# Second input transpose and third output product at other steps of the narrow attention

## The chip, the core and the metric

The kernel runs on one core of one Trainium2 chip. The metric is the device time of one execution, in microseconds (us). The core has a matmul engine (TensorE, PE in the rows; its weight loads are PEld), a vector engine (VectorE, DVE), a scalar engine (ScalarE, ACT), GpSimd (POOL) and SyncE (SP), which issues the DMAs. Each runs its own program in order; semaphores tie them together.

## The reference

Four transformer pieces one after the other on x (4 batches of 512 tokens, width 320) with a context of width 192. The change touches the attentions with 20 heads of 16 columns, which stand in the second piece (a self-attention and a cross-attention) and are the whole of the fourth piece:

```python
h1 = _ln(x, n1_g, n1_b)
x = _attn(h1, h1, q1, k1, v1, o1_w, o1_b, heads) + x
h2 = _ln(x, n2_g, n2_b)
x = _attn(h2, context, q2, k2, v2, o2_w, o2_b, heads) + x
...
q = (x @ wq).reshape(b, n, heads, dh).transpose(0, 2, 1, 3)
k = (ctx @ wk).reshape(b, j, heads, dh).transpose(0, 2, 1, 3)
v = (ctx @ wv).reshape(b, j, heads, dh).transpose(0, 2, 1, 3)
sim = jnp.einsum('bhid,bhjd->bhij', q, k) * scale
a = jax.nn.softmax(sim, axis=-1)
out = jnp.einsum('bhij,bhjd->bhid', a, v)
out = out.transpose(0, 2, 1, 3).reshape(b, n, heads * dh)
return out @ wo + bo
```

## The kernel before

The program is a row of stages: a wide attention (two stages, heads of 64), a feed-forward, the narrow attention of the second piece (two stages, run as one), a feed-forward, a gated attention, and the narrow attention of the fourth piece. `runs` makes two narrow runs: `Run("r3", ...)` with two stages of 4 batches, 8 units n = 0 to 7, and `Run("r7", ...)` with 4 units.

A narrow run is a software pipeline. The functions `narrow_pe`, `narrow_act` and `narrow_dve` each go through rounds n = -1 to N and in a round through 20 steps i (u = i // 4 is a group of four heads, kb = i % 4 a block of 128 keys). A round holds the work of three units: `now` (unit n: scores, exponentials, products with the values), `new` (unit n + 1: its input transposes and its projections) and `old` (unit n - 1: its output projection). A unit with both neighbours is called a full unit below; the first has no `old`, the last no `new`.

The pieces of a step, with the line of the instruction that shows in the trace:
- `cols_pe` (L958): the transposed scores of four heads, four matmuls side by side. It waits for the exponentials of the step before. `exp_act4` (L1003) makes the exponentials on ScalarE.
- `rows_pe4` (L975): scores the other way round, in bf16, of the step 6 later (`LEAD`), for the row maxima; called twice in each step (k = 0 and 1). Each call waits for the count `max`, that is for the VectorE reduction of the call before: `rows_dve4` (L990). Both calls write the same pair of banks.
- at kb = 1 `mix_pe4` (L1033), probabilities times values of the group before, with the first rows call inside; ScalarE copies it to `ox` (L1041). At kb = 2 `negm_pe4` (L1012), a transpose of the maxima, which `negm_dve4` (L1020) adds to the queries. At kb = 3 `turn_pe4` (L1048), transposes of `ox`, which `turn_dve4` reads (L1060, L1062).
- the inputs of the new unit: `T_pe4` (L1107), transposes of its normed (or plain) input in three parts T0, T1, T2, copied by `T_act4` (L1118 or L1120); for cross-attention `C_pe4` (L1129) with C0, C1.
- the output of the old unit: `out_pe4` (L1070), transposes in three parts, copied by `out_act4` (L1078); `y_pe4` (L1086), the output product of the token blocks y0 to y3, three matmuls each with 320 columns. `y_dve4` reads it with the bias added (L1092) and adds it to x (L1095).
- the projections of the new unit: `Q_pe4` (L1151) with the first rows call inside, `K_pe4` (L1178), `V_pe4` (L1204); `Q_act4` (L1160) reads Q0 with two activations.

Everything but the two kinds of scores goes through two PSUM banks, `M.XB` (bank6 and bank7). `step_items` lists the items in the order in which TensorE writes them, and `Turns.__init__` gives them the two banks in turn. So an item's matmuls wait (`wait_free`) until the item two places earlier in that list has been read. `wait_full` is the other direction: the reader waits for the matmuls. Which engine reads an item is fixed: VectorE reads negm, turn and y, ScalarE the others.

The order of the work inside a step is written out by hand, in `narrow_pe`, `narrow_act` and `narrow_dve`, and must agree with `step_items`.

Of the kernel before, what the change touches and what calls it, by code (L numbers as in the profile page):

```python
# [114 lines left out]
def program(nc, io):  # L115
    with ExitStack() as ctx:
# [159 lines left out]
        def overall(s, b):  # L276

            return b + (s.index * B - s.first)
# [140 lines left out]
        def x_ready(eng, s, b):  # L419

            eng.wait_ge(x_done, X_IN + (s.index * B + b) * TB - (B - 1) * TB)
# [482 lines left out]
        class Run(Turns):  # L904


            def step_items(self, n, i):

                u, kb = i // 4, i % 4
                items = []  # L910
                now, new, old = 0 <= n < self.N, n + 1 < self.N, 0 <= n - 1
                if i == 0 and now:
                    items += [("Q2", n), ("V3", n)]
                if kb == 1 and (old if u == 0 else now):
                    items += [("mix%d" % ((u - 1) % 5), n - 1 if u == 0 else n)]
                if kb == 3 and (old if u == 0 else now):
                    items += [("turn%d" % ((u - 1) % 5), n - 1 if u == 0 else n)]
                if i == 2 and now:
                    items += [("K2", n)]
                if i == 3 and new:  # L920
                    items += [("T0", n + 1)]
                if i == 4 and old:
                    items += [("out0", n - 1), ("out1", n - 1)]
                if i == 4 and new:
                    items += [("T1", n + 1)]
                if i == 6 and old:
                    items += [("out2", n - 1)]
                if i == 6 and new:
                    items += [("T2", n + 1)]
                if i == 7 and old:  # L930
                    items += [("y0", n - 1)]
                if i == 7 and new and self.cross[n + 1]:
                    items += [("C0", n + 1)]
                if i == 8 and new and self.cross[n + 1]:
                    items += [("C1", n + 1)]
                if i == 8 and old:
                    items += [("y1", n - 1), ("y2", n - 1)]
                if i == 11 and old:
                    items += [("y3", n - 1)]
                if new:  # L940
                    items += {10: [("Q0", n + 1)], 12: [("K0", n + 1)], 14: [("V0", n + 1)], 15: [("V1", n + 1)], 16: [("Q1", n + 1)],
                              18: [("K1", n + 1)], 19: [("V2", n + 1)]}.get(i, [])
                if kb == 2 and (new if u == 4 else now):
                    items += [("negm%d" % ((u + 1) % 5), n + 1 if u == 4 else n)]
                return items
# [152 lines left out]
        def T_pe4(pe, r, n, c):  # L1098
            (s, b), item, (a, w) = r.work[n], f"T{c}", CH3[c]
            r.wait_free(pe, item, n)  # L1100
            if c == 0 and s.prm["ln"]:
                pe.wait_ge(xn, TB * (overall(s, b) + 1))
            if c == 0 and not s.prm["ln"]:
                x_ready(pe, s, b)
            for t in range(TB):
                src = M.xn[:, t, a:a + w] if s.prm["ln"] else M.x[:, b * TB + t, a:a + w]
                last = nc.tensor.transpose(r.bank_of(item, n)[0:w, t * P:t * P + P], src, M.ident[:, :])  # L1107
            last.then_inc(r.full(item, n), 1)
# [108 lines left out]
        def narrow_pe(pe, r):  # L1217
            start(pe, r.work[0][0], r.work[0][1])
            for n in range(-1, r.N + 1):
                now, new, old = 0 <= n < r.N, n + 1 < r.N, 0 <= n - 1  # L1220
                for i in range(20):
                    u, kb = i // 4, i % 4
                    if now:
                        cols_pe(pe, r, n, i)
                    if i == 0 and now:
                        Q_pe4(pe, r, n, 2, n, i)
                        V_pe4(pe, r, n, 3)
                    elif i == 1 and old:
                        mix_pe4(pe, r, n - 1, 4, i)
                    elif kb == 1 and now and u:  # L1230
                        mix_pe4(pe, r, n, u - 1, i)
                    elif i == 2 and now:
                        K_pe4(pe, r, n, 2, n, i)
                    elif i == 3:
                        if old:
                            turn_pe4(pe, r, n - 1, 4)
                        rows_pe4(pe, r, n, i, 0)
                        if new:
                            T_pe4(pe, r, n + 1, 0)
                    elif i == 4:  # L1240
                        if old:
                            out_pe4(pe, r, n - 1, 0)
                            out_pe4(pe, r, n - 1, 1)
                        rows_pe4(pe, r, n, i, 0)
                        if new:
                            T_pe4(pe, r, n + 1, 1)
                    elif i == 6:
                        if old:
                            out_pe4(pe, r, n - 1, 2)
                        rows_pe4(pe, r, n, i, 0)  # L1250
                        if new:
                            T_pe4(pe, r, n + 1, 2)
                    elif i == 7:
                        if now:
                            turn_pe4(pe, r, n, 0)
                        rows_pe4(pe, r, n, i, 0)
                        if old:
                            y_pe4(pe, r, n - 1, 0)
                        if new and r.cross[n + 1]:
                            C_pe4(pe, r, n + 1, 0)  # L1260
                    elif i == 8:
                        if new and r.cross[n + 1]:
                            C_pe4(pe, r, n + 1, 1)
                        if old:
                            y_pe4(pe, r, n - 1, 1)
                        rows_pe4(pe, r, n, i, 0)
                        if old:
                            y_pe4(pe, r, n - 1, 2)
                    elif i == 10 and new:
                        Q_pe4(pe, r, n + 1, 0, n, i)  # L1270
                    elif i == 11:
                        if now:
                            turn_pe4(pe, r, n, 1)
                        rows_pe4(pe, r, n, i, 0)
                        if old:
                            y_pe4(pe, r, n - 1, 3)
                    elif i == 12 and new:
                        K_pe4(pe, r, n + 1, 0, n, i)
                    elif i == 14 and new:
                        rows_pe4(pe, r, n, i, 0)  # L1280
                        V_pe4(pe, r, n + 1, 0)
                    elif i == 15:
                        if now:
                            turn_pe4(pe, r, n, 2)
                        rows_pe4(pe, r, n, i, 0)
                        if new:
                            V_pe4(pe, r, n + 1, 1)
                    elif i == 16 and new:
                        Q_pe4(pe, r, n + 1, 1, n, i)
                    elif i == 18 and new:  # L1290
                        K_pe4(pe, r, n + 1, 1, n, i)
                    elif i == 19:
                        if now:
                            turn_pe4(pe, r, n, 3)
                        rows_pe4(pe, r, n, i, 0)
                        if new:
                            V_pe4(pe, r, n + 1, 2)
                    else:
                        rows_pe4(pe, r, n, i, 0)
                    if kb == 2 and u < 4 and now:  # L1300
                        negm_pe4(pe, r, n, u + 1)
                    if i == 18 and new:
                        negm_pe4(pe, r, n + 1, 0)
                    rows_pe4(pe, r, n, i, 1)

        def narrow_act(act, r):
            start(act, r.work[0][0], r.work[0][1])
            for n in range(-1, r.N + 1):
                now, new, old = 0 <= n < r.N, n + 1 < r.N, 0 <= n - 1
                for i in range(20):  # L1310
# [14 lines left out]
                    if i == 4 and old:  # L1325
                        out_act4(act, r, n - 1, 0)
                        out_act4(act, r, n - 1, 1)
                    if i == 4 and new:
                        T_act4(act, r, n + 1, 1)
                    if i == 6 and old:  # L1330
                        out_act4(act, r, n - 1, 2)
# [27 lines left out]
        def narrow_dve(dve, r):  # L1359
# [7 lines left out]
            for n in range(-1, r.N + 1):  # L1367
                now, new, old = 0 <= n < r.N, n + 1 < r.N, 0 <= n - 1
                norm = ln and n + 2 <= r.N
                for i in range(20):  # L1370
# [13 lines left out]
                    if i == 7 and old:  # L1384
                        s = r.work[n - 1][0]
                        dve.wait_ge(s.sem("cols_in"), 48 if s.prm["ln"] else 16)
                        y_dve4(dve, r, n - 1, 0)
                    if i == 8 and old:
                        y_dve4(dve, r, n - 1, 2)
                    if i == 11 and old:  # L1390
                        y_dve4(dve, r, n - 1, 3)
# [647 lines left out]
```

## Time and profile before

| | us |
|---|---|
| median of three runs | 3612.92 |
| lowest and highest run | 3609.6 and 3615.88 |
| profiled execution: measured time | 3612.91 |
| profiled execution: span from the first to the last instruction | 3611.0 |
| TensorE busy | 3419.9 (95%) |
| VectorE busy | 1909.7 (53%) |
| ScalarE busy | 1483.3 (41%) |
| GpSimd busy | 677.3 (19%) |

The run of 8 units begins with its first input transposes at 1923.3 us of the span and its last ones start by 2579.6; those of the run of 4 units lie between 3188.2 and 3437.2. In a timeline row the first number is the start, the second the length, both in us; several instructions of one kind that follow one another are one row, with their count. A bracket tells how long the engine had been idle and what ended that.

### The profile page before, as it was taken

To read this page: it belongs to the slowest core of one execution; us is meant where nothing else is said; L and a number is where in the kernel's file an instruction comes from. 1 tells how busy PE (TensorE), PEld (TensorE's weight loads), DVE (VectorE), ACT (ScalarE), POOL (GpSimd) and SP (SyncE) were. 2 spreads that over 40 slices of the span, in tenths; PEclk is the share of its full clock that TensorE was granted. 3 is DMA by queue.
4 is the path that set the end of the run, shared out by engine and by line. 5 is a ranking of instruction groups with operands and counts; after the bars stand their busy time and mean duration, and the time that the engine had idled before them with its cause. 6 is when DMAs were issued, how large, how long until landed. Compare 5 with 4: busy or idle time off the path is not lost.

```text
span 3611.0 us, 38848 instructions
## 1 busy us (share of the span) xinstructions
PE 3419.9 (95%) x15478; PEld 1418.8 (39%) x15478; DVE 1909.7 (53%) x2246; ACT 1483.3 (41%) x2023; POOL 677.3 (19%) x420
## 2 busy tenths in 40 slices
PE   8999999999999999999996899999998999989997
PEld 3334343433334343434443333333333545633332
DVE  3656556565656566661222666666661222556663
ACT  3443434344444535331110555556552112326553
POOL 2433333343333433330000000000000000000000
PEclk9999999999999999999997999999999999979999
DMA  3000000000100000002000000000003000000000
GB/s 109 19 15 15 19 15 15 21 17 21 33 18 15 21 12 15 15 1 57 0 0 24 1 1 1 21 10 5 1 1 80 1 0 23 1 5 5 5 1 30
DMA packets 43554, 60.49 MB, mean 17 GB/s; under 512 B 7408, under 2 KB 31216, under 8 KB 43376
## 3 DMA queue, kind: packets, MB, share of 16 engines
q1 hardware_dynamic: 43376, 58.02, 5.5%
q8 instruction: 124, 2.03, 0.2%
q14 instruction: 54, 0.44, 0.0%
HBM read 55.39 MB, written 2.62 MB: 16 GB/s over the span
## 4 chain that ended last, share of the span: by engine, by line
PE 89%; DVE 5%; issue 3%; ACT 2%; DMA 1%; SPq 1%; POOL 0%; ACTq 0%; DVEq 0%; POOLq 0%
PE bank L463 9%; PE bank L551 9%; PE bank L1033 6%; PE bank L673 5%; PE bank L348 5%; PE bank L1485 4%; PE bank L609 4%; PE bank L958 4%; PE bank L975 4%; PE bank L1487 4%; PE bank L1151 3%; PE bank L612 3%; DVE heads L990 3%; PE bank L644 2%; PE bank L1086 2%
## 5 line engine op out<-in xcount | busy, mean ns | idle before, releaser
L990 DVE TENSOR_REDUCE heads<-bank 128x2 f32<-128x1024 f32 x480 | 587.5, 1224 | 426.9 <-PE bank L975 425.7
L500 DVE TENSOR_REDUCE heads<-bank 128x2 f32<-128x1024 f32 x320 | 390.9, 1222 | 534.9 <-PE bank L488 531.2
L522 ACT ACTIVATE probs<-bank 128x1024 f32<-128x1024 f32 x320 | 327.6, 1024 | 425.8 <-PE bank L468 423.0
L535 POOL TENSOR_TENSOR heads<-heads,probs 128x1024 f32<-128x1024 f32 x160 | 381.2, 2382 | 254.8 <-ACT probs L522 252.2
L463 PE MATMUL bank<-heads 64*128 64x512 f32 x1280 | 361.3, 641 | 0.9 <-ACT probs L522 0.9
L551 PE MATMUL bank<-probs,values 128*64 128x512 f32 x1280 | 345.2, 618 | 0.2 <-ACT probs L522 0.2
L531 POOL TENSOR_TENSOR heads<-probs 128x1024 f32<-128x1024 f32 x80 | 193.1, 2413 | 749.2 <-ACT probs L522 749.2
L958 PE MATMUL bank<-heads 32*128 32x512 f32 x1920 | 306.5, 624 | 5.9 <-ACT weights L1003 3.0
L580 DVE RECIPROCAL rec<-ox 128x128 f32<-128x128 f32 x320 | 280.1, 917 | 7.7 <-ACT ox L573 7.7
L1003 ACT ACTIVATE weights<-bank 128x1024 f32<-128x1024 f32 x238 | 230.6, 1021 | 114.5 <-PE bank L958 113.9
L975 PE MATMUL bank<-heads 32*128 32x512 bf16 x960 | 191.7, 396 | 62.8 <-DVE heads L990 57.9
L1509 ACT ACTIVATE probs<-bank,b_col 128x512 f32<-128x512 f32 x80 | 55.0, 687 | 455.5 <-PE bank L1488 455.5
L1520 DVE SCALAR_TENSOR_TENSOR mixed<-bank,b_col,probs 128x512 f32<-128x512 f32 x80 | 60.0, 750 | 299.4 <-ACT probs L1509 299.4
L1169 POOL CAST heads<-heads 128x512 bf16<-128x512 f32 x60 | 36.2, 625 | 928.4 <-ACT heads L1160 928.4
L1003 ACT ACTIVATE probs<-bank 128x1024 f32<-128x1024 f32 x164 | 158.9, 1021 | 74.6 <-PE bank L958 73.9
L463 PEld LDWEIGHTS bank<-heads 64*128 64x128 f32 x1280 | 96.3, 184 | 223.0 <-issue 111.6
L348 PE MATMUL bank<-weights,mixed 128*128 128x320 f32 x640 | 173.7, 433 | 3.3 <-DVE mixed L1520 3.3
L975 PEld LDWEIGHTS bank<-heads 32*128 32x128 bf16 x960 | 46.0, 91 | 324.9 <-DVE heads L990 186.4
L586 DVE TENSOR_TENSOR mixed<-mixed,rec 128x512 f32<-128x512 f32 x62 | 168.4, 2716 | 0.1
L1485 PE MATMUL bank<-hT,weights 128*128 128x512 f32 x320 | 161.6, 628 | 6.2 <-DMA weights<-in_L_xattn_w_ff 3.1
L609 PE MATMUL bank<-hT,heads 128*128 128x512 f32 x320 | 160.1, 623 | 0.0
L1487 PE MATMUL bank<-hT,weights 128*128 128x512 f32 x320 | 152.5, 599 | 0.0
(202 smaller groups left out, 4819.2 us busy)
## 6 DMA issues: line engine op xcount, KB each, us to landing
heads<-in_wqk SPq DMA_DIRECT2D x40, 320.0 KB, 2.8
heads<-in_wqk SPq DMA_DIRECT2D x40, 256.0 KB, 2.6
ctx_in<-in_ctx SPq DMA_DIRECT2D x12, 384.0 KB, 3.7
weights<-in_L_xattn_wo SPq DMA_DIRECT2D x2, 1600.0 KB, 11.1
x_res<-in_x SPq DMA_DIRECT2D x4, 640.0 KB, 11.9
out<-x_res SPq DMA_DIRECT2D x1, 2560.0 KB, 8.7
weights<-in_L_xattn_w_ff SPq DMA_DIRECT2D x1, 1600.0 KB, 13.2
weights<-in_L_xattn_ff_w SPq DMA_DIRECT2D x1, 1600.0 KB, 14.5
```

Of the source, the lines that this page charges most:

```text
L348: last = nc.tensor.matmul(M.SM[t % 2][:, 0:D], v["OT"][:, c, t * P:t * P + P], v["wo"][:, c, :], start=c == 0, stop=c == NF - 1)
L463: nc.tensor.matmul(M.COLS[:, g, :], v["KT"][strip, U % 3, kb * P:kb * P + P], v["QT"][strip, U % 3, :], start=True, stop=False)
L500: nc.vector.tensor_reduce(v["negm"][:, U % 2, qb, :].rearrange("p (g k) -> p g k", g=2)[:, :, 0], M.ROWS[:, :, :], AX.X, ALU.max, negate=T ...
L522: nc.scalar.activation(v["probs"][:, kb, :, :], M.COLS[:, :, :], ACT.Exp, scale=float(r.work[n][0].prm["dh"]) ** -0.5).then_inc(r.sem("exp ...
L535: nc.gpsimd.tensor_tensor(ps, ps, pr[:, k, :, :], ALU.add).then_inc(r.sem("part"), 1)
L551: last = nc.tensor.matmul(M.WOB[64 * g:64 * g + 64, :], v["V"][:, kb, 2 * u + g, :], v["probs"][:, kb, g, :], start=kb == 0, stop=kb == TB ...
L609: last = nc.tensor.matmul(q[:, :], w[:, e, :], M.hT[:, e, :], start=False, stop=e == 1)
L958: last = nc.tensor.matmul(M.QUAD[:, g, :], v["KT"][strip, u, kb * P:kb * P + P], v["QT"][strip, u, :], start=True, stop=True)
L975: last = nc.tensor.matmul(M.ROWS4[:, j, :], v["QB"][strip, u, qb * P:qb * P + P], v["KB"][strip, u, :], start=True, stop=True)
L990: nc.vector.tensor_reduce(v["negm"][:, tile, qb, 64 * half:64 * half + 64].rearrange("p (g k) -> p g k", g=2)[:, :, at], M.ROWS4[:, :, :], ...
L1003: nc.scalar.activation(v["probs"][g % slots][:, 2 * h:2 * h + 2, :], M.QUAD[:, 2 * h:2 * h + 2, :], ACT.Exp, scale=float(r.work[n][0].prm[ ...
L1485: nc.tensor.matmul(gate[:, :], v["w1"][:, e, gf], M.hT[:, e, :], start=e == 0, stop=False)
```

## The change

The transposes T1 of the new unit are issued in step 5, behind the mix matmuls, instead of in step 4, behind the first rows call; their ScalarE copy moves with them. The output product y2 of the old unit is issued in step 10, behind the query projection and ahead of the negm transposes, instead of in step 8, between the two rows calls; on VectorE its two additions go from step 8 to step 10, behind the negm addition. `step_items` lists both at their new places, and with that the two banks change for the items between the old place and the new one. No operation is added or removed.

```diff
@@ step_items
-                if i == 4 and new:
+                if i == 5 and new:
                     items += [("T1", n + 1)]
...
                 if i == 8 and old:
-                    items += [("y1", n - 1), ("y2", n - 1)]
+                    items += [("y1", n - 1)]
...
+                if i == 10 and old:
+                    items += [("y2", n - 1)]
                 if kb == 2 and (new if u == 4 else now):
@@ narrow_pe
                         rows_pe4(pe, r, n, i, 0)
-                        if new:
-                            T_pe4(pe, r, n + 1, 1)
                     elif i == 6:
...
                         if old:
                             y_pe4(pe, r, n - 1, 1)
                         rows_pe4(pe, r, n, i, 0)
+                    elif i == 10:
+                        if new:
+                            Q_pe4(pe, r, n + 1, 0, n, i)
+                        else:
+                            rows_pe4(pe, r, n, i, 0)
                         if old:
                             y_pe4(pe, r, n - 1, 2)
-                    elif i == 10 and new:
-                        Q_pe4(pe, r, n + 1, 0, n, i)
...
+                    if i == 5 and new:
+                        T_pe4(pe, r, n + 1, 1)
                     if kb == 2 and u < 4 and now:
                         negm_pe4(pe, r, n, u + 1)
@@ narrow_act
-                    if i == 4 and new:
+                    if i == 5 and new:
                         T_act4(act, r, n + 1, 1)
@@ narrow_dve
-                    if i == 8 and old:
+                    if i == 10 and old:
                         y_dve4(dve, r, n - 1, 2)
```

What this does to the queues is shown for round n = 1 of the run of 8 units. In the new file the helpers' lines are 2 higher (L958 is L960, L975 is L977, L1086 is L1088, and so on), and L1398 is L1403. A row is an instruction of the queue, with its bank and the semaphores that it waits for; r3_free0 and r3_free1 count the readings of bank6 and bank7, r3_max the reductions.

TensorE, from the first rows call of step 4 to that of step 5, before:

```order
L975 MATMUL bank4<-heads 128x512 [waits r3_max]
...
L1107 MATMUL bank6<-ident,xn 106x128 [waits r3_free0]
L1107 MATMUL bank6<-ident,xn 106x128 x3
L975 MATMUL bank4<-heads 128x512 [waits r3_max]
...
L1033 MATMUL bank7<-weights,values 32x512 [waits r3_exp,r3_free0,r3_free1]
L1033 MATMUL bank7<-weights,values 32x512 x3
```

And now, to the end of step 5:

```order
L977 MATMUL bank4<-heads 128x512 [waits r3_max]
...
L1035 MATMUL bank6<-weights,values 32x512 [waits r3_exp,r3_free0]
L1035 MATMUL bank6<-weights,values 32x512 x3
...
L1035 MATMUL bank6<-mixed,values 32x512 x4
L1109 MATMUL bank7<-ident,xn 106x128 [waits r3_free1]
L1109 MATMUL bank7<-ident,xn 106x128 x3
L977 MATMUL bank4<-heads 128x512 [waits r3_max]
```

T1 has gone from between the two rows calls of step 4 to the end of mix0, and mix0 and T1 have changed banks.

TensorE in steps 10 and 11, from the query projection Q0 to y3, before:

```order
L1151 MATMUL bank6<-hT,weights 128x512 x2
L1012 MATMUL bank7<-ident,heads 128x128 [waits r3_max,r3_free1]
L1012 MATMUL bank7<-ident,heads 128x128 x3
L975 MATMUL bank4<-heads 128x512 [waits r3_max]
...
L1048 MATMUL bank6<-ident,ox 128x128 [waits r3_free1,r3_free0]
L1048 MATMUL bank6<-ident,ox 128x128 x3
...
L1086 MATMUL bank7<-weights,mixed 128x320 [waits s3_wo_in,r3_free0,r3_free1]
```

And now:

```order
L1153 MATMUL bank7<-hT,weights 128x512 x2
L1088 MATMUL bank6<-weights,mixed 128x320 [waits s3_wo_in,r3_free0]
L1088 MATMUL bank6<-weights,mixed 128x320 x2
L1014 MATMUL bank7<-ident,heads 128x128 [waits r3_max,r3_free1]
L1014 MATMUL bank7<-ident,heads 128x128 x3
L977 MATMUL bank4<-heads 128x512 [waits r3_max]
...
L1050 MATMUL bank6<-ident,ox 128x128 [waits r3_free0]
L1050 MATMUL bank6<-ident,ox 128x128 x3
```

y2 stands between Q0 and the negm transposes. The negm transposes now follow Q0 in bank7, and the turn transposes (L1050) follow y2 in bank6, where they followed Q0 before.

VectorE from the second rows call of step 10 to the first of step 11, before:

```order
L990 TENSOR_REDUCE heads<-bank4 128x2 [waits r3_rows]
L1020 TENSOR_TENSOR heads<-bank7,heads 128x512 [waits r3_q_cast,r3_full1]
L1398 BN_STATS stats<-x_res 128x6
L990 TENSOR_REDUCE heads<-bank4 128x2 [waits r3_rows]
L1060 RECIPROCAL rec<-bank6 128x16 [waits r3_free1,r3_full0]
```

And now:

```order
L992 TENSOR_REDUCE heads<-bank4 128x2 [waits r3_rows]
L1022 TENSOR_TENSOR heads<-bank7,heads 128x512 [waits r3_q_cast,r3_full1]
L1094 TENSOR_TENSOR ysum<-bank6,bo_row 128x320 [waits r3_full0]
L1097 TENSOR_TENSOR x_res<-ysum,x_res 128x320 [waits r3_free0]
L1403 BN_STATS stats<-x_res 128x6
```

The reading of y2 stands behind the reduction and behind the negm addition.

## Rows read from the trace of the kernel before

**Rows 1.** The page: the chain that ended last, by engine

```profile
PE 89%; DVE 5%; issue 3%; ACT 2%; DMA 1%; SPq 1%; POOL 0%; ACTq 0%; DVEq 0%; POOLq 0%
```

**Rows 2.** Stretches: us, then PE, PEld, DVE, ACT, POOL busy, clock, DMA

```profile
2100.00:2188.00 88.00, 84.06 (x520) 33.49 (x524) 59.05 (x77) 50.76 (x61) 6.60 (x12) 1.00 0.00 1
```

**Rows 3.** L1107 on PE: idle until, us in total, times

```profile
  ACT mixed L1078: 9.5, 8
```

**Rows 4.** Timeline of PE, round 1, steps 4 and 5

```profile
2102.32 1.15 PE L958 MATMUL bank<-heads 32*128 32x512 f32 x8
...
2105.98 0.65 PE L1107 MATMUL bank<-ident,xn 128*106 128x128 f32 x4 [1.18 <-ACT mixed L1078]
...
2106.57 1.24 PE L958 MATMUL bank<-heads 32*128 32x512 f32 x8
...
2111.77 1.24 PE L958 MATMUL bank<-heads 32*128 32x512 f32 x8
```

**Rows 5.** Timeline of PE, round 7 (no new unit), step 4

```profile
2659.94 1.14 PE L958 MATMUL bank<-heads 32*128 32x512 f32 x8
...
2663.74 0.39 PE L975 MATMUL bank<-heads 32*128 32x512 bf16 x2 [1.32 <-DVE heads L990]
```

**Rows 6.** Timeline of PE, round 0 (no old unit), behind T1 in step 4

```profile
2013.38 0.39 PE L975 MATMUL bank<-heads 32*128 32x512 bf16 x2 [0.75 <-DVE heads L990]
```

**Rows 7.** Timeline of PE and DVE, round 1, step 8

```profile
2123.30 0.39 PE L975 MATMUL bank<-heads 32*128 32x512 bf16 x2
...
2123.62 1.89 PE L1086 MATMUL bank<-weights,mixed 108*128 108x320 f32 x6
2123.73 1.23 DVE L990 TENSOR_REDUCE heads<-bank 128x2 f32<-128x1024 f32 x1 [0.84 <-PE bank L975]
2124.87 0.48 DVE L1092 TENSOR_TENSOR ysum<-bank,bo_row 128x320 f32<-128x320 f32 x1
...
2125.43 0.39 PE L975 MATMUL bank<-heads 32*128 32x512 bf16 x2
```

**Rows 8.** Timeline of all engines, round 1, steps 10 and 11

```profile
2133.19 1.98 PE L1151 MATMUL bank<-hT,weights 106*128 106x512 f32 x4
...
2135.01 0.60 PE L1012 MATMUL bank<-ident,heads 128*128 128x128 f32 x4
...
2135.30 1.44 ACT L1160 ACTIVATE heads<-bank,mask 128x512 f32<-128x512 f32 x2 [1.36 <-PE bank L1151]
...
2135.55 1.24 PE L958 MATMUL bank<-heads 32*128 32x512 f32 x8
2135.98 1.23 DVE L990 TENSOR_REDUCE heads<-bank 128x2 f32<-128x1024 f32 x1 [1.38 <-PE bank L975]
...
2136.80 0.66 PE L1048 MATMUL bank<-ident,ox 128*128 128x128 f32 x4
...
2137.12 0.68 DVE L1020 TENSOR_TENSOR heads<-bank,heads 128x512 f32<-128x512 f32 x1
...
2137.86 1.89 PE L1086 MATMUL bank<-weights,mixed 108*128 108x320 f32 x6
...
2139.68 1.24 PE L958 MATMUL bank<-heads 32*128 32x512 f32 x8
```

**Rows 9.** Timeline of PE, round 7, steps 10 and 11

```profile
2687.35 1.24 PE L958 MATMUL bank<-heads 32*128 32x512 f32 x8
...
2690.93 0.39 PE L975 MATMUL bank<-heads 32*128 32x512 bf16 x2 [0.80 <-DVE heads L990]
...
2695.05 1.24 PE L958 MATMUL bank<-heads 32*128 32x512 f32 x8
```

**Rows 10.** Round 0, step 9: the stretch, and timeline of PE

```profile
2029.00:2037.00 8.00, 7.88 (x48) 1.85 (x50) 2.52 (x3) 1.94 (x2) 0.00 (x0) 0.65 0.01 2
...
2029.13 2.31 PE L958 MATMUL bank<-heads 32*128 32x512 f32 x8
...
2036.91 1.24 PE L958 MATMUL bank<-heads 32*128 32x512 f32 x8
```

## The prediction

> **What bounds the kernel now.** I read the chain that ended last first: TensorE holds 89% of it [rows 1], so the kernel is one engine's program with holes, and a moved piece of TensorE work is worth what it does to the holes. The stretch-by-stretch view comes next: in a stretch of 88 us, about one middle unit of the narrow attention, TensorE is busy 84.06 us at a granted clock of 1.00, against 59.05 on VectorE and 50.76 on ScalarE [rows 2]. So nothing but TensorE has slack there, but TensorE's holes, some 4 us in a unit, are waits for the other two engines. Then I read one unit as a timeline. Its steps are counted by the scores matmuls (L958). Every step has two "rows" matmuls (L975), each answered by a reduction on VectorE (L990), and the second one has to wait for the reduction of the first. That pair is the second clock of a step: where little else stands between them, TensorE waits for VectorE; where much stands between them, it doesn't.
>
> Which units feel the change: T1 belongs to a unit that has a next one, y2 to a unit that has a previous one. The run of two attentions (8 units) has one unit with only a next (the first, beside a start-up round), six with both and one with only a previous; the run of the last attention (4 units) has one, two and one. So there are 8 full units, 2 first and 2 last ones. The wait list of T's line confirms the count: eight waits for a copy on L1078, 9.5 us together [rows 3].
>
> **Part 1, T1 leaves step 4.** Now step 4 lasts from 2102.32 to 2106.57, 4.25 us, and in it the transposes wait 1.18 us for ScalarE's copy of out0 [rows 4]. That wait goes, but not its whole length comes back, because the second rows matmul then waits for VectorE. The last unit of the run has no T1 and shows the same step without it: its second rows matmul starts 3.80 us after the scores and waits 1.32 us for VectorE [rows 5]; with 0.01 to the next scores the step is 3.81. So the gain is 4.25 - 3.81 = 0.44 us in each full unit, not 1.18 + 0.65. In a first unit there is no out0 and T1 stands beside the VectorE wait: its second rows matmul still waits 0.75 us behind T1 [rows 6], so nothing is gained there.
>
> **Part 2, T1 enters step 5.** It stands behind the last mix matmul and ahead of the second rows matmul. That step has no hole at its end: from 2106.57 to 2111.77 it lasts 5.20 us with no wait on the rows [rows 4]. So T1 costs its own time, 0.59 us (2105.98 to 2106.57) [rows 4], in full and first units alike. Its ScalarE copy comes after the copy of mix0 and ahead of the next exponentials, which by the same shift start later than the copy ends; I cost it at nothing. Bounds for this part: 0.59 to 0.65, the bare length of the four transposes.
>
> **Part 3, y2 leaves step 8.** Between the two rows matmuls of step 8 now stand the three y2 products: 2123.30 to 2125.43, 2.13 us. Without them the second waits for the reduction, which ends at 2123.73 + 1.23 = 2124.96; with 0.06 for the hand-over (as between ScalarE's end at 2136.74 and the transposes at 2136.80 [rows 8]) the start is 2125.02, a gain of 0.41 us out of 1.81 [rows 7]. The next reduction may not start earlier, as VectorE is by then at y1's two additions (from 2124.87) [rows 7], but the first mix matmuls of step 9 stand between it and the next rows matmul. The gain holds in 8 full and 2 last units.
>
> **Part 4, y2 enters step 10.** The step now is the query projection (L1151), the negm transposes (L1012) and the second rows matmul, back to back: 2133.19, 2135.01, 2135.55 [rows 8]. TensorE is the late one, so y2 costs what it takes in step 8: 2123.62 to 2125.43, 1.81 us [rows 7]. The order also makes negm3 share its bank with Q0. Q0 would be full 0.41 us earlier than now, so its two ScalarE passes end at 2135.30 + 1.44 - 0.41 = 2136.33, and y2 ends at 2135.01 - 0.41 + 1.81 = 2136.41. A tie: I take 0, and bound it by 0 to 0.3 us.
>
> **Part 5, step 11 gets a new wait.** With two banks in turn, an item waits until the item two places earlier has been read. Now turn1 follows Q0 in its bank, and ScalarE has read Q0 by 2136.74, when turn1 starts 1.25 us after the scores (2135.55 to 2136.80) [rows 8]. In the new order turn1 follows y2 in its bank, and y2 is read by VectorE, in the queue behind the second reduction of step 10 and the negm3 addition. Counted from the scores of step 11: reduction starts at +0.43 (2135.55 to 2135.98), negm3 addition +1.14 later (to 2137.12), then +0.60 (its 0.68 with the same 0.08 of overlap) [rows 8], the addition of y2 0.48 [rows 7], hand-over 0.06: 2.71 us. turn1 starts 1.46 us later than now. Behind it stand the first rows matmul, y3 and the second one. y3's present wait of some 0.15 us for the negm3 addition (2137.12 + 0.68 against its start at 2137.86) [rows 8] goes, so the step gets 1.46 - 0.15 = 1.31 us longer. The scores of step 11 are ahead of turn1, so ScalarE isn't starved, and nothing later in the unit is timed by anything but this chain; the delay stays.
> The Trainium skill, "PSUM — Partial Sum Buffer", section "Engine vs sequencer instructions", says that the VectorE queue is strict FIFO, which speaks against this place for y2. By that rule part 5 stands at 1.31; if VectorE could take y2 ahead of the waiting reduction it would be 0 and the time about 3627.7.
>
> **Sum.** Full unit: -0.44 + 0.59 - 0.41 + 1.81 + 1.31 = +2.86 us, times 8 = 22.9. First units: 0.59 x 2 = 1.2. Last units: -0.41, then step 10, where y2 first fills the 0.80 us that the second rows matmul waits there [rows 9], +1.81 - 0.80 = 1.01, then step 11 as before, from the same 4.12 us (2690.93 to 2695.05) [rows 9], +1.31: 1.91 x 2 = 3.8. Together +27.9 us. The profiled execution took 3612.91 us (span 3611.0), which is the median of the three runs, 3612.92; so the forecast is 3640.8 us, 0.77% slower.
>
> **Rivals.**
> *No wait in step 11.* If the hand-over of y2 to VectorE were not late (for instance if the reduction of step 10 is already done when turn1 comes), part 5 goes in 10 units: 27.9 - 13.1 = 14.8, so 3627.7. For it speaks only that such a wait isn't to be seen in the profile before; against it stands the order of VectorE's queue.
> *The moved work is hidden and the kernel gets faster.* This is the case if steps 5 and 10 have as much room on TensorE as the moved pieces take, 0.59 and 1.81 us, and y2 is read in time. Then only the gains are left: -0.85 x 8 - 0.41 x 2 = -7.6, so 3605.3. It decides at the point where another engine sets the length of those steps. The timeline speaks against it: TensorE's instructions follow one another there without a wait [rows 4, 8].
> *The clock falls.* In a first unit one step shows a granted clock of 0.65, so TensorE was for most of it at the lower of its two levels (1.2 and 2.4 GHz) [rows 10]: a step that normally lasts 5.20 us (2106.57 to 2111.77) [rows 4] took 7.78 (2029.13 to 2036.91) [rows 10], +2.58. If the new 1.46 us wait did this once in each full unit, it would add 20.6 us: 3661.4. Against it: full units have waits of 1.18 us now and run at 1.00 [rows 2, 4], and the new wait stands between busy steps. Where the clock falls already, in first and last units, the moment may shift; I allow one such step, 2.58 us, either way.
> The Trainium skill, "TensorE: Matmul & The Clock Gate", section "A second HAM failure mode: psum-queue depth-cycling", tells of a kernel whose short waits at PSUM banks made its clock swing between the levels; in this trace the full units, with waits of just that kind, don't.
>
> **How the numbers follow.** Forecast 0.82 (own range 3634 to 3647: the tie of part 4 up to +2.4, part 2 up to +0.6, the clock 2.6, and as much downwards for overlaps that I read too tightly); no wait in step 11 0.07; clock 0.05; faster 0.03; within 0.2% for reasons that I don't see 0.03. The range runs from 3627, to take in the first rival, to 3650, one or two falls of the clock beyond the forecast. Within 0.2%, 7 us, a measurement of this kernel can't tell a change from none. Faster 0.03, same 0.03, slower 0.94.
>
> **What the changed profile would show.** Right: T's line has no waits for L1078 left; step 4 of a full unit lasts 3.8 us and step 5 5.8; step 8 4.7 us instead of 5.1; step 10 6.7 instead of 4.9; step 11 5.4 instead of 4.1, with turn1 (the transposes of ox) waiting about 1.4 us for VectorE's y addition; a full unit grows by 2.9 us. Wrong: turn1 waits for ScalarE or not at all; the second rows matmul of step 8 moves by the whole 1.81 us; steps 5 and 10 keep their length; a granted clock under 1.00 in the middle units; or waits later in the unit that shrink by what step 11 lost.

## The result, and the profile after

The changed kernel takes 3642.22 us (median of 6 runs, 3639.7 to 3646.07) against 3612.72 us for the kernel before in the same rounds: a ratio of 1.0082 with a 95% interval of 1.0069 to 1.0095. It is slower, as forecast; 3640.8 us had been predicted. The profiled execution's span grew from 3611.0 to 3639.2 us, by 28.2.

| step of round 1 (from scores to scores) | before | forecast | after |
|---|---|---|---|
| 4 | 4.25 | 3.81 | 3.81 |
| 5 | 5.20 | 5.79 | 5.79 |
| 8 | 5.13 | 4.72 | 4.71 |
| 10 | 4.91 | 6.72 | 6.74 |
| 11 | 4.13 | 5.44 | 5.43 |

The page of the changed kernel, busy time by engine and the chain that ended last:

```profile
PE 3422.2 (94%) x15478; PEld 1419.1 (39%) x15478; DVE 1908.0 (52%) x2246; ACT 1483.4 (41%) x2023; POOL 674.5 (19%) x420
...
PE 89%; DVE 5%; issue 3%; ACT 1%; DMA 1%; SPq 0%; POOL 0%; ACTq 0%; DVEq 0%; POOLq 0%
```

TensorE does the same work in a longer span; the chain is TensorE's as before [rows 1]. Its timeline in round 1 answers to [rows 4, 7, 8]. In it the scores are L960, the rows matmuls L977, T L1109, y L1088 and the turn transposes L1050. Steps 4, 5 and 8:

```profile
2104.15 1.14 PE L960 MATMUL bank<-heads 32*128 32x512 f32 x8
...
2107.96 0.39 PE L977 MATMUL bank<-heads 32*128 32x512 bf16 x2 [1.33 <-DVE heads L992]
...
2107.96 1.24 PE L960 MATMUL bank<-heads 32*128 32x512 f32 x8
...
2113.17 0.65 PE L1109 MATMUL bank<-ident,xn 128*106 128x128 f32 x4
...
2113.75 1.24 PE L960 MATMUL bank<-heads 32*128 32x512 f32 x8
...
2122.28 1.24 PE L960 MATMUL bank<-heads 32*128 32x512 f32 x8
...
2125.27 0.39 PE L977 MATMUL bank<-heads 32*128 32x512 bf16 x2
2125.70 1.23 DVE L992 TENSOR_REDUCE heads<-bank 128x2 f32<-128x1024 f32 x1 [0.84 <-PE bank L977]
...
2126.99 0.39 PE L977 MATMUL bank<-heads 32*128 32x512 bf16 x2 [1.33 <-DVE heads L992]
...
2126.99 1.24 PE L960 MATMUL bank<-heads 32*128 32x512 f32 x8
```

Both steps from which something was taken now hold a wait of 1.33 us for VectorE, where the moved work stood. The places that it went to, steps 10 and 11:

```profile
2132.20 1.24 PE L960 MATMUL bank<-heads 32*128 32x512 f32 x8
...
2136.56 1.78 PE L1088 MATMUL bank<-weights,mixed 108*128 108x320 f32 x6
...
2136.85 1.45 ACT L1162 ACTIVATE heads<-bank,mask 128x512 f32<-128x512 f32 x2 [1.36 <-PE bank L1153]
...
2138.35 0.66 PE L1014 MATMUL bank<-ident,heads 128*128 128x128 f32 x4
...
2138.94 1.24 PE L960 MATMUL bank<-heads 32*128 32x512 f32 x8
2139.36 1.23 DVE L992 TENSOR_REDUCE heads<-bank 128x2 f32<-128x1024 f32 x1 [3.21 <-PE bank L977]
...
2140.51 0.68 DVE L1022 TENSOR_TENSOR heads<-bank,heads 128x512 f32<-128x512 f32 x1
2141.11 0.48 DVE L1094 TENSOR_TENSOR ysum<-bank,bo_row 128x320 f32<-128x320 f32 x1
...
2141.64 0.66 PE L1050 MATMUL bank<-ident,ox 128*128 128x128 f32 x4 [1.46 <-DVE ysum L1094]
...
2144.37 1.24 PE L960 MATMUL bank<-heads 32*128 32x512 f32 x8
```

The turn transposes wait 1.46 us for the reading of y2, whose row (L1094) stands behind the reduction and the negm addition. VectorE had stood idle for 3.21 us when that reduction began at 2139.36, though y2's matmuls were over by 2138.34 (2136.56 + 1.78): it waited for the instruction that came first in its program, and y2 was read at 2141.11. The list of what the turn transposes waited for in the whole run, releaser, us in total and times, shows that it is every unit with an old one, 8 full and 2 last:

```profile
  DVE ysum L1094: 14.6, 10
```

**Unit by unit.** I took the starts of all scores matmuls of the narrow runs from both traces and subtracted step lengths. Six of the eight full units grew by 2.85 to 2.87 us, through steps 4, 5, 8, 10 and 11 alone. The other two (rounds 2 and 6) grew by 4.5, for in their step 11 the granted clock fell. Together the full units grew by 26.1 us, where 22.9 were forecast. The first units grew by 3.7 and 2.2, together 6.0 against 1.2; step 5 has 2.16 of it in both, and the rest of the 3.7 is the clock in other steps (0, 2, 9 and 12), in which the first unit of the run of 8 differs from trace to trace. The last units grew by 1.9 and 1.7, 3.6 against 3.8. That is 35.7 us inside the units. Outside them the new trace is 7.5 us shorter than the old one: 1.9 ahead of the first unit's scores, 3.2 between the two runs, 2.4 behind the last unit. Apart from the start-up and draining rounds of the narrow runs, the work there is in stages with not an instruction changed; the 2.4 us behind the last unit are missing in five of the eight other traces too, with the change and without it, and are there in three. So I take the 7.5 us for a difference between two executions. The good agreement of the total owes something to them; the step lengths above don't.

### The profile page after: what moved, and what is told of

Read it like the earlier page. It is cut to its first block, busy times and chain, and to the rows that moved or that the text cites. A ratio compares the mean times of both kernels' runs of the same rounds, so it can differ in the third digit from the quotient of the medians.

```text
span 3639.2 us, 38848 instructions
## 1 busy us (share of the span) xinstructions
PE 3422.2 (94%) x15478; PEld 1419.1 (39%) x15478; DVE 1908.0 (52%) x2246; ACT 1483.4 (41%) x2023; POOL 674.5 (19%) x420
## 4 chain that ended last, share of the span: by engine, by line
PE 89%; DVE 5%; issue 3%; ACT 1%; DMA 1%; SPq 0%; POOL 0%; ACTq 0%; DVEq 0%; POOLq 0%
PE bank L463 9%; PE bank L551 9%; PE bank L1035 6%; PE bank L673 5%; PE bank L348 5%; PE bank L1490 4%; PE bank L609 4%; PE bank L977 4%; PE bank L960 4%; PE bank L1492 4%; DVE heads L992 3%; PE bank L1153 3%; PE bank L612 3%; PE bank L644 2%; PE bank L1088 2%
## 5 line engine op out<-in xcount | busy, mean ns | idle before, releaser
L960 PE MATMUL bank<-heads 32*128 32x512 f32 x1920 | 308.0, 627 | 5.9 <-ACT weights L1005 3.0
L977 PE MATMUL bank<-heads 32*128 32x512 bf16 x960 | 193.0, 398 | 85.7 <-DVE heads L992 80.8
L977 PEld LDWEIGHTS bank<-heads 32*128 32x128 bf16 x960 | 46.0, 91 | 344.7 <-DVE heads L992 203.7
## 6 DMA issues: line engine op xcount, KB each, us to landing
x_res<-in_x SPq DMA_DIRECT2D x4, 640.0 KB, 12.7
```

The costliest lines, as they stand in the source:

```text
L960: last = nc.tensor.matmul(M.QUAD[:, g, :], v["KT"][strip, u, kb * P:kb * P + P], v["QT"][strip, u, :], start=True, stop=True)
L977: last = nc.tensor.matmul(M.ROWS4[:, j, :], v["QB"][strip, u, qb * P:qb * P + P], v["KB"][strip, u, :], start=True, stop=True)
```

## The experiments

Lengths are from one trace each; ratios are against the kernel before, which ran between them on the same chip (3611.73 us median beside the first three, 3610.73 with all its runs).

**T1 alone.** From the kernel before:

```diff
-                if i == 4 and new:
+                if i == 5 and new:
                     items += [("T1", n + 1)]
...
-                        if new:
-                            T_pe4(pe, r, n + 1, 1)
                     elif i == 6:
...
+                    if i == 5 and new:
+                        T_pe4(pe, r, n + 1, 1)
...
```

(and the same step for the ScalarE copy in `narrow_act`).

> The kernel before with T1 alone moved to step 5; y2 stays in step 8. By the terms of the prediction: step 4 of a full unit 0.44 us shorter, step 5 0.59 longer, in first units only the 0.59: +0.15 x 8 + 0.59 x 2 = +2.4 us over the kernel before. Second theory (the clock): taking T1 out of step 4 of a first unit leaves TensorE emptier there, and the clock falls in step 5, as the changed kernel's trace shows in the last attention's first unit (+2.16 us instead of +0.59): +2.4 + 2 x 1.57 = +5.5 us. Rival (T1 carries the loss, since it changes which items share a bank): more than +14 us.

Measured: 3616.56 us, ratio 1.0015 (1.0005 to 1.0024), that is 1.8 to 8.7 us slower; 2.4 us had been expected by the prediction's terms, 5.5 with the clock. All eight full units show -0.44 in step 4 and +0.57 or +0.58 in step 5, +0.14 in sum; the two first units show +2.22 and +2.17 in step 5. So T1 costs about what its step lengths say, 8 x 0.14 + 4.4 = 5.5 us, four fifths of it in the first units. The big loss isn't T1's.

**y2 alone.** The changed kernel with the T1 edits of the diff undone (the y2 lines of the diff stay).

```diff
-                if i == 5 and new:
+                if i == 4 and new:
                     items += [("T1", n + 1)]
...
```

(and so in `narrow_pe` and `narrow_act`).

> The kernel before with y2 alone moved to step 10; T1 stays in step 4. By the terms of the prediction: full units -0.41 + 1.81 + 1.31 = +2.71 us, 8 of them 21.7; last units +1.91 x 2 = 3.8; together +25.5 us over the kernel before, with the turn transposes waiting 1.46 us for the reading of y2 in 10 steps. With two falls of the clock in step 11, as in the changed kernel's trace, some 3 more. Rival (the two moves only cost so much together, because the bank order changes over the whole stretch between them): under +14 us.

Measured: 3637.53 us, 25.8 over the kernel before; ratio 1.008 (1.0061 to 1.0098). Seven full units grew by 2.71 to 2.73 us; in the eighth (round 2 of the last attention) the clock fell in step 11 and it grew by 4.37. The turn transposes waited for y2's reading in the same 10 places, 14.6 us. The two parts add up within the noise (4.8 and 25.8 us against 29.5), and y2 carries almost nine tenths.

**The reading of y2 put first.** TensorE's program and the banks are those of the changed kernel; only VectorE's order in step 10 is another:

```diff
+                    if i == 10 and old:
+                        y_dve4(dve, r, n - 1, 2)
                     rows_dve4(dve, r, n, i, 1)
...
-                    if i == 10 and old:
-                        y_dve4(dve, r, n - 1, 2)
```

> The changed kernel with one VectorE order altered: in step 10 y2 is read ahead of the second reduction, not behind it and the negm addition. TensorE's order and the banks stay. If the wait of the turn transposes is the place in VectorE's queue: the reading ends about 2.2 us earlier, the 1.46 us wait goes, step 11 falls from 5.43 to about 4.2 us in 10 units, so 12 us faster than the changed kernel and, without the falls of the clock behind that wait, 15: +13 to +16 us over the kernel before. If the wait came from the shared bank as such, whatever VectorE's order is: no change against the changed kernel, +29.

Measured: 3628.9 us, ratio 1.0052 (1.0035 to 1.0069), faster than the changed kernel by 13 us between the medians and 11 by the ratios. It is 17.2 us over the kernel before, a little more than the 13 to 16 expected; the step lengths give 12.7 us in the full units, 4.4 in step 5 of the first ones and 1.1 in steps 8, 10 and 11 of the last ones, 18.2 together. Step 11 is as long as in the kernel before, within 0.04 us, in seven full units (0.21 longer in one) and 0.17 longer in the two last ones; step 10 of a full unit keeps its +1.84. The timeline of all engines in round 1:

```profile
2137.82 0.49 DVE L1094 TENSOR_TENSOR ysum<-bank,bo_row 128x320 f32<-128x320 f32 x1 [2.23 <-PE bank L1088]
...
2138.81 1.23 DVE L992 TENSOR_REDUCE heads<-bank 128x2 f32<-128x1024 f32 x1
...
2139.55 0.66 PE L1050 MATMUL bank<-ident,ox 128*128 128x128 f32 x4
```

VectorE had been idle for 2.23 us when y2 came, read it at once, and was free for the reduction when that was due, 0.43 us behind the rows matmul. The turn transposes start 1.17 us after the scores (2138.38) and wait for nothing. The bank they share with y2 is the same; so the 1.31 us of step 11 were the place in VectorE's queue.

**The reading of y2 put later still.** The opposite dose, behind the batch-norm statistics of step 10:

```diff
-                    if i == 10 and old:
-                        y_dve4(dve, r, n - 1, 2)
...
                             norm_apply(t, at)
+                    if i == 10 and old:
+                        y_dve4(dve, r, n - 1, 2)
```

> The changed kernel with the reading of y2 put still later in VectorE's queue of step 10: behind the batch-norm statistics instruction too, which takes 0.48 us there in rounds 1 to 6 of the run of 8 units, and doesn't exist in the run of 4. If the wait of the turn transposes is counted by what stands ahead of y2 in that queue: 1.46 us becomes 1.94 and step 11 0.5 us longer in those six rounds (+3 us over the changed kernel), and both stay as they are in the last attention's units. If the wait has another cause: the same step 11 everywhere.

Measured: 3644.64 us in one run, whose total is too little to tell 2 or 3 us. Step 11 is 1.70 us longer than in the kernel before, instead of 1.31, in five of the six rounds that have the statistics instruction; in the sixth (round 1) the clock fell in that step and it is 3.59 longer. In the units of the last attention, which have none, it stays at +1.31. The wait is 1.85 us (timeline of VectorE and TensorE, round 2):

```profile
2242.58 0.48 DVE L1401 BATCH_NORM_STATS2 stats<-x_res 128x6 f32<-128x320 f32 x1
2242.98 0.47 DVE L1094 TENSOR_TENSOR ysum<-bank,bo_row 128x320 f32<-128x320 f32 x1
...
2243.51 0.66 PE L1050 MATMUL bank<-ident,ox 128*128 128x128 f32 x4 [1.85 <-DVE ysum L1094]
```

The dose arrives, 0.39 us instead of the 0.48 expected: the statistics row begins at 2242.58 and the next at 2242.98, so 0.40 is what it adds to the queue, and its own length, which I had used, is 0.08 more than that.

**T1 back in step 4 in first units only.** The changed kernel, with `old` deciding where T1 stands:

```diff
-                if i == 5 and new:
+                if i == (5 if old else 4) and new:
                     items += [("T1", n + 1)]
...
```

(and the same condition in `narrow_pe` and `narrow_act`).

> The changed kernel with T1 back in step 4 in the first units alone (no old unit). By the prediction's term: 0.59 x 2 = 1.2 us less than the changed kernel. By the theory that the emptier step 4 of a first unit lets the clock fall in step 5: step 5 of those units is 5.2 us long again, with a granted clock of 1.00 in it, and lasts 2.16 us less than in the changed kernel; about 4.3 us for both. The step lengths of the trace tell the two apart, the total time hardly.

Measured: 3646.56 us in one run, which tells nothing at this size, as was said: its first units lost time to the lower clock in steps 0 and 2. The step in question is settled. Step 5 of the first units is +0.22 us against the kernel before in the run of 8 units and +0.00 in the last attention. In both, all four traces with T1 out of step 4 (changed kernel, T1 alone, y2 read first, y2 read later) have +2.11 to +2.22. The stretch 3272 to 3280 of the last attention's round 0, with the columns of [rows 2], in the changed kernel:

```profile
3272.00:3280.00 8.00, 6.95 (x45) 1.61 (x46) 3.45 (x3) 2.81 (x4) 0.00 (x0) 0.79 0.00 0
```

The changed kernel's timeline of TensorE there, in which step 5 begins with the scores of 3273.06:

```profile
3271.34 0.39 PE L977 MATMUL bank<-heads 32*128 32x512 bf16 x2 [0.47 <-DVE heads L992]
3273.05 0.39 PE L977 MATMUL bank<-heads 32*128 32x512 bf16 x2 [1.33 <-DVE heads L992]
3273.06 1.24 PE L960 MATMUL bank<-heads 32*128 32x512 f32 x8
3274.23 1.90 PE L1035 MATMUL bank<-probs,values 128*32 128x512 f32 x8
...
3279.85 0.65 PE L1109 MATMUL bank<-ident,x_res 128*106 128x128 f32 x4
```

With T1 back between the two rows matmuls, the same stretch:

```profile
3272.00:3280.00 8.00, 6.79 (x60) 1.91 (x54) 4.90 (x4) 4.35 (x5) 0.00 (x0) 1.00 0.01 3
```

and its timeline of TensorE:

```profile
3273.36 0.39 PE L977 MATMUL bank<-heads 32*128 32x512 bf16 x2 [0.47 <-DVE heads L992]
3273.68 0.65 PE L1109 MATMUL bank<-ident,x_res 128*106 128x128 f32 x4
3275.07 0.39 PE L977 MATMUL bank<-heads 32*128 32x512 bf16 x2 [0.74 <-DVE heads L992]
...
3276.25 1.07 PE L1035 MATMUL bank<-probs,values 128*32 128x512 f32 x8
```

With T1 there TensorE waits 0.74 us, without it 1.33, and the same eight mix matmuls behind it take 1.07 us at a granted clock of 1.00 or 1.90 in a stretch at 0.79, part of it at the lower of the two levels (1.2 and 2.4 GHz). The slow mix matmuls (3274.23) come ahead of T1's new place in step 5 (3279.85), so it is what left step 4 that lowers the clock, and not what came into step 5. In a first unit T1's transposes cost nothing in step 4, and their absence costs 2.16 - 0.59 = 1.57 us in step 5.

**The same lesson at y0.** From the kernel before, VectorE's order in step 7 alone:

```diff
+                    if i == 7 and old:
+                        s = r.work[n - 1][0]
+                        dve.wait_ge(s.sem("cols_in"), 48 if s.prm["ln"] else 16)
+                        y_dve4(dve, r, n - 1, 0)
                     rows_dve4(dve, r, n, i, 1)
```

(with the same four lines taken away behind it).

> The kernel before, with the same idea at another place: in step 7 VectorE reads y0 ahead of the second reduction. In full units whose new unit is of a cross-attention the second context transposes wait 0.86 us for that reading in step 8. If VectorE's order is what such a wait costs, it goes: step 8 0.86 us shorter in 6 units, 5.2 us less than the kernel before; no step of the other units changes. If TensorE then meets another wait at the same place, step 8 shrinks by less.

Measured: 3607.51 us in one run, 3.2 below the median of the kernel before, whose own runs beside it spread from 3604.8 to 3615.04; so the total shows nothing here, and the step lengths have to. Step 8 is 0.85 to 0.87 us shorter in exactly the six units with a cross-attention ahead, and no step of the other full units changed. The wait of the context transposes (L1129), in the kernel before

```profile
  DVE ysum L1092: 5.2, 6
```

in total and times, is gone from the list.

**Two moves in the kernel before.** The y0 order, and out1 instead of T1 taken out of step 4:

```diff
                 if i == 4 and old:
-                    items += [("out0", n - 1), ("out1", n - 1)]
+                    items += [("out0", n - 1)]
...
+                if i == 5 and old:
+                    items += [("out1", n - 1)]
...
                             out_pe4(pe, r, n - 1, 0)
-                            out_pe4(pe, r, n - 1, 1)
...
+                    if i == 5 and old:
+                        out_pe4(pe, r, n - 1, 1)
...
```

(and the copy of out1 likewise in `narrow_act`).

> The kernel before with two moves: y0 read ahead of the second reduction of step 7 (-0.86 us in 6 units, -5.2), and in the place of T1 the output transpose out1 moved, from step 4 to the end of step 5, with T1 left between the rows matmuls of step 4. By the lesson of T1: what must leave step 4 is something ahead of the first rows matmul, since between the two rows matmuls VectorE's 1.7 us are spent anyway; T1 (0.59 us) then stands in that time and waits for nothing, since its bank was read long before. Step 4 of a full unit 4.25 - 0.54 - 0.44 = 3.27 us, step 5 +0.54, together -0.44 in 8 units, -3.5. Sum -8.7 us, 3603 or a ratio of 0.9976. Rival (the clock): an emptier step 4 lets the clock fall in step 5 of some units, +1.6 us each, and takes most of the gain back.

Measured: 3600.28 us, ratio 0.9974 (0.9965 to 0.9983), faster than both kernels. TensorE in round 1, step 4:

```profile
2100.83 1.14 PE L960 MATMUL bank<-heads 32*128 32x512 f32 x8
2101.90 0.65 PE L1072 MATMUL bank<-ident,mixed 128*108 128x128 f32 x4
2102.48 0.39 PE L977 MATMUL bank<-heads 32*128 32x512 bf16 x2
2102.80 0.65 PE L1109 MATMUL bank<-ident,xn 128*106 128x128 f32 x4
2104.19 0.39 PE L977 MATMUL bank<-heads 32*128 32x512 bf16 x2 [0.75 <-DVE heads L992]
2104.20 1.24 PE L960 MATMUL bank<-heads 32*128 32x512 f32 x8
```

T1 waits for nothing and stands inside VectorE's time. Step 4 is 0.87 us shorter in every full unit and step 5 0.58 longer, -0.29 in sum instead of -0.44: out1 had cost only 0.44 us behind out0 and costs 0.58 alone. Step 8 gives its 0.86 in the six units. By step lengths that is -7.5 us in the full units; the last units lose 0.15 each in steps 4 and 5, and the clock fell in none of the full ones. The rest up to the measured -10.4 isn't attributed.

**ScalarE's order in step 6 too.** The kernel just shown, with

```diff
+                    if i == 6 and old:
+                        out_act4(act, r, n - 1, 2)
                     if now:
                         exp_act4(act, r, n, i)
...
```

(and the same call taken away behind the exponentials).

> The kernel of the run before this one (y0 read first, out1 later) with one ScalarE order altered too: in step 6 out2 is copied ahead of the exponentials, not behind them. The negm transposes of step 6 now wait 1.05 us for that copy, in 8 full units. Expected: that wait goes; but the exponentials start about 1.1 us later, and the third and fourth scores matmuls of step 7 wait for them; step 6 gets 0.8 to 1.0 us shorter and step 7 0.3 to 0.6 longer, net -0.3 to -0.5 us in 8 units, about -3 more, 3600. Rival: ScalarE's exponentials become the late ones and nothing is gained or up to 0.3 us lost in each unit.

Measured: 3597.94 us, ratio 0.997 (0.996 to 0.998), which this measurement can't tell from the run before it. Its step lengths can: step 6 is 0.82 or 0.83 us shorter in seven units, and step 7 0.40 longer in rounds 1 and 2 and 0.62 to 0.64 in those with a cross-attention ahead, so the gain is 0.2 to 0.4 us a unit. In one unit it is 0.48 and 0.29. Half to three quarters of what step 6 gave was lost again in step 7, as expected from exponentials that start later.

## Why the prediction was right, step by step

Parts 1 to 5 held in the full units to 0.03 us each: -0.44, +0.58 (0.59 forecast), -0.42 (0.41), +1.84 (1.81), +1.31. What made that possible was that each term came from two instants of the same unit, and that the two ends of each moved piece were asked separately: what is late next where it leaves, and what it costs where it lands.

The tie in part 4, negm3 against ScalarE's reading of Q0, came out as a tie: the negm transposes have no wait in their own row, and step 10 grew by 1.84 us where y2's cost alone was put at 1.81.

Part 5 hangs on the order of VectorE's queue, and the two runs on the place of y2 show it: with y2's reading earlier in the queue step 11 grows by 0 us, in the changed kernel by 1.31, one instruction later by 1.70. The Trainium skill, "PSUM — Partial Sum Buffer", section "Engine vs sequencer instructions", calls that queue strict FIFO; these three lengths agree.

One small term of the last units was off: their step 10 grew by 0.80 us, not 1.01. The prediction took y2 at its 1.81 us and the negm transposes at the 0.66 of their row; in the changed kernel's unit 7 the negm transposes begin 1.73 us behind y2's start and the next rows matmul 0.53 behind theirs.

Two larger terms were mis-sized, both by the clock. The first is part 2 in first units: 0.59 us was the cost of T1's time, and step 5 grew by 2.16 in both. I had called T1's leaving of step 4 worth nothing there, since its time was hidden beside a wait; it was hidden, but it also kept TensorE from standing idle, and four of four traces without it show the fall, none of the others (T1 back in those units: +0.22 and 0.00). The error is 1.57 us in each of two units.

The second is the clock rival, to which I gave 0.05 as a fall in every full unit and which came true in part. In the four traces in which the turn transposes wait 1.46 us or more for y2, the clock fell in step 11 of 5 of 32 full units (two, one, one, one), at 1.6 to 1.7 us of the unit's length in four of them (4.37 to 4.51 against 2.71 to 2.87) and 3.2 in the fifth (6.48 against 3.25, spread over steps 11 and 12). One last unit of the changed kernel shows it too, +2.26 in step 11 in place of +1.31. In the six traces without that wait (the kernel before, T1 alone, y2 read first, y0 read first, and the last two) step 11 of 48 full units shows no such fall; the largest deviation is 0.21 us. In the changed kernel, round 2, the stretches:

```profile
2236.00:2242.00 6.00, 4.54 (x22) 2.23 (x20) 4.93 (x8) 1.94 (x2) 0.78 (x2) 0.84 0.00 1
2242.00:2248.00 6.00, 6.00 (x27) 2.23 (x28) 3.95 (x6) 2.39 (x3) 0.00 (x0) 0.87 0.00 0
```

and its timeline of TensorE there:

```profile
2238.53 0.66 PE L1050 MATMUL bank<-ident,ox 128*128 128x128 f32 x4 [1.46 <-DVE ysum L1094]
...
2239.44 2.96 PE L1088 MATMUL bank<-weights,mixed 108*128 108x320 f32 x6
```

The same wait and the same rows stand in the neighbouring units, where y3 takes 1.88 us and not 2.96. So a fall behind this wait is possible, not certain; what decides in which unit it happens stays open. The Trainium skill, "TensorE: Matmul & The Clock Gate", section "A second HAM failure mode: psum-queue depth-cycling", which I had set against the trace of before, is borne out here in a weak form: a fall in 5 of 32 units.

These two, 3.1 and 3.2 us, are more than the 2.6 that the range allowed for the clock, and would have put the forecast at 3647. The profiled run (3641.07) lies below that because the rest of the program ran 7.5 us shorter in it; the other five runs, from 3639.7 to 3646.07, have no trace. That the median of 3642.2 lies so near 3640.8 is luck to that extent. The rival without a wait in step 11 gave 3627.7 us, and the run that took that wait away gave 3628.9; by its step lengths it should lie at 18.2 us over the kernel before, not 14.8, most of the difference being the fall in step 5 of the first units.

## What to carry to other kernels

A wait that ends with another engine gives back only what the next-late engine leaves: where two instructions have a reduction between them, work between the two is free as long as it fits into the wait for the reduction, and work ahead of the first isn't, so move the latter. When a buffer's turn order puts an item behind one that another engine reads, count that engine's queue up to the reading; reordering the reader (y2, y0) lengthened no other step of a full unit and gave 1.3 and 0.86 us a unit, where moving the producer lost. Work that is hidden in a wait may still be keeping the matmul clock up.

## What the runs showed of the hardware that I had not expected

Removing 0.6 us of transposes that were hidden in a wait lowered the granted clock one step later, reproducibly: +2.11 to +2.22 us in eight of eight first units, against 0.00 to 0.22 with the transposes in place. And VectorE's rows overlap by 0.08 or 0.09 us where the second need not wait for the first: the negm addition starts 1.15 us behind a reduction of 1.23 (2139.36 to 2140.51), and the statistics row of 0.48 us adds 0.40 to the queue.
